# Rounded parts for two value projections and one value output product, with VectorE's sums made around them, in a cross-attention kernel on one Trainium2 core

## What is computed

```
Q = (img_embed @ Wq)          # 4096 x 512, heads of 512
K = (sent_embed @ Wk)         # 2 x 77 rows of 384
V = (sent_embed @ Wv)
score = einsum('bhqd,bhkd->bhqk', Q, K) / sqrt(512)
attn = softmax(where(mask, score, -inf))
ctx = einsum('bhqk,bhkd->bqhd', attn, V)
out = ctx @ Wo + img_embed
out = (out - mean) * rsqrt(var + 1e-5) * gamma + beta
```

## Time and profile before

| | us |
|---|---|
| median of 3 runs | 355.23 |
| profiled execution | 355.34 |
| its span in the trace | 353.3 |
| TensorE matmul busy | 347.6 (98%) |
| TensorE weight load busy | 324.0 (92%) |
| VectorE busy | 278.0 (79%) |
| ScalarE busy | 233.9 (66%) |
| GpSimd busy | 192.8 (55%) |

### The profile page before, as it was taken

The page is one execution under the profiler, slowest core; times in us unless marked ns, Lnnn a source line. Parts: engine busy times, 40 slices in busy tenths (PEclk is TensorE's granted clock), DMA queues, the critical chain, the costliest instruction groups (busy, mean ns, idle before and its releaser), DMA issues. The chain is left out here.

```text
span 353.3 us, 6822 instructions
## 1 busy us (share of the span) xinstructions
PE 347.6 (98%) x2272; PEld 324.0 (92%) x2272; DVE 278.0 (79%) x513; ACT 233.9 (66%) x784; POOL 192.8 (55%) x208
## 2 busy tenths in 40 slices
PE   9999999999999999999999999999999999999994
PEld 6999999999999999998899899989988998999884
DVE  2159999579756468898798988987987989889896
ACT  3267764254555669877876976878778769768560
POOL 0045650000003857689669688688696796885243
PEclk9999999999999999999999999999999999999998
DMA  7998769875635070053242341441522423413012
GB/s 250 414 420 316 272 225 339 262 267 221 217 131 220 0 283 17 4 178 105 76 160 63 136 151 46 164 144 38 179 97 83 151 70 138 149 42 110 32 47 103
DMA packets 19683, 55.80 MB, mean 158 GB/s; under 512 B 1729, under 2 KB 3265, under 8 KB 17729
## 3 DMA queue, kind: packets, MB, share of 16 engines
q1 hardware_dynamic: 18784, 54.38, 42.6%
q10 hardware_dynamic: 864, 1.00, 0.9%
HBM read 46.98 MB, written 8.39 MB: 157 GB/s over the span
## 5 line engine op out<-in xcount | busy, mean ns | idle before, releaser
L663 PE MATMUL pair<-vw_hi,pt_hi 128*128 128x512 f32 x155 | 62.3, 402 | 0.0
L663 PE MATMUL pair<-vw_hi,pt_lo 128*128 128x512 f32 x155 | 60.8, 393 | 0.0
L663 PE MATMUL pair<-vw_lo,pt_hi 128*128 128x512 f32 x155 | 60.6, 391 | 0.0
L1281 POOL TENSOR_TENSOR out_sb<-centred,beta_sb 128x512 f32<-128x512 f32 x30 | 38.8, 1294 | 29.0 <-ACT centred L857 28.9
L1301 POOL TENSOR_TENSOR x_sum<-xt_in 128x256 f32<-128x256 f32 x16 | 11.9, 745 | 62.2 <-DMA xt_in<-x_tiles 62.0
L812 ACT ACTIVATE prob<-c,neg_max 128x77 f32<-128x77 f32 x128 | 43.9, 346 | 0.0
L1326 POOL TENSOR_TENSOR xo_lo<-x_sum,xo_hi 128x512 fp32r<-128x512 f32 x32 | 41.4, 1298 | 0.5 <-ACT xo_hi L836 0.5
L588 PE MATMUL pair<-a_hi,xo_hi 128*128 128x308 f32 x128 | 40.4, 315 | 0.0
L588 PE MATMUL pair<-a_hi,xo_lo 128*128 128x308 f32 x128 | 38.9, 304 | 0.0
L588 PE MATMUL pair<-a_lo,xo_hi 128*128 128x308 f32 x128 | 38.9, 304 | 0.0
L1123 DVE TENSOR_TENSOR pair<-pair,x_in 128x512 f32<-128x512 f32 x31 | 21.7, 699 | 21.0 <-PE pair L663 20.7
(11 more groups left out here) (120 smaller groups left out, 992.7 us busy)
## 6 DMA issues: line engine op xcount, KB each, us to landing
w_out<-wo SPq DMA_DIRECT2D x8, 1024.0 KB, 4.8
xt_in<-x_tiles SPq DMA_DIRECT2D x16, 512.0 KB, 3.9
x_in<-x_rows SPq DMA_DIRECT2D x16, 512.0 KB, 4.8
out<-out_sb SPq DMA_DIRECT2D x31, 256.0 KB, 2.2
w_out<-wq_t SPq DMA_DIRECT2D x7, 1024.0 KB, 7.5
w_proj<-wv SPq DMA_DIRECT2D x8, 768.0 KB, 4.7
w_proj<-wk SPq DMA_DIRECT2D x6, 768.0 KB, 9.2
w_out<-wq_t SPq DMA_DIRECT2D x2, 512.0 KB, 7.5
```

What stands on the lines that cost most here:

```text
L663: mm = pe.matmul(ps_out[:, i % 2, 0:s.model], ps[:, j, :], v[:, b, j, :], start=(j == 0 and n == 0), stop=(j == s.key_t - 1 and n == len(p ...
L1281: pool.tensor_tensor(out_sb[i % OUT_RING][:, :], centred[i % 2][:, :], beta_sb[:, :], ALU.add)\
```

## The change

Projections 8 and 9 (values 0 and 1) and output product 8 are now done of rounded parts. `SPLIT_VALUES` gains use 8 (`H`), and projections are whole again from use 10 (`FROM_FULL`) instead of 8. Output product 9 stays whole although its projection comes in two pieces, so VectorE adds the second piece to `v_t` (`add_kv`), and TensorE waits for that sum (`dve_kv_sum`). VectorE makes T1 of batch 0 ahead of those additions and T1 of batch 1 behind them; T2 follows after output product 8's additions. ScalarE and GpSimd run their existing helpers for the added uses.

```
-    SPLIT_VALUES = range(H + 4, USES - 1)
+    SPLIT_VALUES = (H, *range(H + 4, USES - 1))
+    FROM_FULL = H + 2
...
-            return u < FULL_PROJ or u >= H
+            return u < FULL_PROJ or u >= FROM_FULL
...
+        def summed_kv(u):
+
+            return whole_out(u) and not whole(u)
...
             def wait_kv(u, half):
 
-                if whole_out(u):
+                if summed_kv(u):
+                    pe.wait_ge(dve_kv_sum, 2 * sum(summed_kv(v) for v in range(u)) + half + 1)
+                elif whole_out(u):
                     pe.wait_ge(act_kv_hi, 2 * u + half + 1)
...
+            def add_kv(u):
+
+                for half in range(2):
+                    values = value_of(u)[:, 2 * half:2 * half + 2, :]
+                    dve.wait_ge(act_kv_hi, 2 * u + half + 1)
+                    dve.tensor_tensor(values, second(ps_proj[half]), values, ALU.add).then_inc(dve_kv_sum, 1)
...
             for u in range(USES):
+                if u == H:
+                    right_sum(T1, 0)
                 if u + 1 < USES and not whole_out(u + 1):
                     split_kv(u + 1)
+                elif u + 1 < USES and summed_kv(u + 1):
+                    add_kv(u + 1)
+                if u == H:
+                    right_sum(T1, 1)
...
-                for n, task in {H: ((T1, right_sum), (T2, right_sum)), H + 1: ((T1, split_t), (T4, right_sum)),
+                for n, task in {H: ((T2, right_sum),), H + 1: ((T1, split_t), (T4, right_sum)),
...
-            for u in range(FULL_PROJ, H):
+            for u in range(FULL_PROJ, FROM_FULL):
```

More of the change, by code:

```diff
@@ L252, in build @@
         dve_comb, dve_half_max = sem("dve_comb"), sem("dve_half_max")
-        dve_vw_sum = sem("dve_vw_sum")
+        dve_vw_sum, dve_kv_sum = sem("dve_vw_sum"), sem("dve_kv_sum")
         dve_centred, dve_pad, dve_last = sem("dve_centred"), sem("dve_pad"), sem("dve_last")
```

## The result

| | before | after |
|---|---|---|
| median of the executions timed side by side, us | 355.3 (354.82 to 355.81, 6) | 356.8 (356.34 to 356.99, 6) |
| profiled execution, us | 355.34 | 356.77 |
| its span, us | 353.3 | 354.9 |
| last matmul of the program starts, us | 348.10 | 349.72 |

The ratio is 1.004 (95% interval 1.0027 to 1.0053): slower by 1.5 us. The forecast was 357.2 in a range of 356.0 to 358.4.

A forecast was written before the change was run, and what follows sets the result against it. TensorE was taken to bound the kernel, its saving swallowed by a wait for VectorE's vw_lo. Profiled 355.34 + 1.9 = 357.25, from the median 357.1; forecast 357.2 us, range 356.0 to 358.4.

The forecast's parts named there:

- TensorE's saving: Two split projections 0.24, one split output product 0.17, one mode change 0.02: TensorE spared 0.43 us at most.
- The 2.6 us: By the skill's four-pass rule the 40 replaced products would save 2.6 us on TensorE; the prediction kept the trace's 0.43.
- Step 1: VectorE's w_out_lo pairs, uses 6 and 7: with GpSimd newly working beside them, 3.50 us instead of 2.27.
- Step 2: VectorE, use 7: full rounds of 7.09 us move the instruction at 66.11 to 68.61, a delay of 2.50 us.
- Step 3: VectorE, use 8: four additions put among the T1 and T2 sums cost 1.29 us, bounds 1.2 and 1.92.
- Step 4: VectorE, end of T2: the splitting of T1 starts at 79.23 instead of 77.20, remaining delay 2.03 us.
- Step 5: VectorE from 77.20 to vw_lo: no idle time, so the vw_lo subtractions end at 91.66 instead of 89.63.
- The term +1.9: TensorE, second half of projection 12: waits for vw_lo and goes on at 91.74 instead of 89.81, +1.9 us.
- The short waits: Projection 10 waits for kv(9)'s sum (72.50 against 72.23); output product 9 finds its sums about on time; total unchanged.
- The clock rival: In TensorE's stall the granted clock falls too, costing 1.8 us or more: 359.1 us; chance 0.12.
- Not slower: GpSimd doesn't hold VectorE's w_out_lo: vw_lo 0.55 late, TensorE 0.4, 355.7 us; chance 0.12 with the still faster cases.

The follow-up runs named there:

- experiments 3 and 4: Changed kernel, each: GpSimd clearing w_proj_lo of projections 8 and 9 (355.56 us); vw_lo ahead of one sum plus v_t additions ahead of T1 (354.54 us).
- Experiment 3: Changed kernel with GpSimd writing zeros into w_proj_lo of projections 8 and 9 instead of subtracting: 355.56 us, ratio 1.0012.

## Why the prediction was right, step by step

- **TensorE's saving, 0.43.** It measured 0.42: from projection 7 to projection 12 TensorE takes 37.20 us before and 36.78 in the two kernels that have all the new products and no wait for `v_t` (experiments 3 and 4). In the changed kernel it takes 37.04, as 0.26 is given back in front of projection 10. (Projection 12 starts 0.26 us earlier on the clock of the span, but 0.10 of that is an earlier start of the whole chain.) The 2.6 us that the prediction worked out from the Trainium skill ("FP8 and Floating Point Precision", TensorE Precision Notes) showed in none of the versions without a wait for `vw_lo` (354.84, 354.54, 354.73): by it they would have come near 352.6. For the whole product the four passes fit: 4 x 154 columns at 2.4 GHz are an estimated 0.257 us, and its row gives 0.262. It is the rounded pair that the estimate had too cheap: 462 columns at one a cycle would be an estimated 0.193 us, and it takes 0.253.
- **Step 1, GpSimd's hold.** From the start of the pair to the next instruction 3.45 and 3.49 us, where 3.50 was forecast; the first instruction took 2400 ns. Experiment 3 shows that it is GpSimd's instruction, and that about 1.1 us of the run hang on it. The Trainium skill ("SBUF — State Buffer", Who interferes with whom) says that a VectorE instruction with two inputs in SBUF contends with a GpSimd instruction that reads SBUF, and that the shared ports are an exclusive lock. The trace agrees as to the contention: `w_out_lo` took 2400 ns where GpSimd was still subtracting, and both instructions of a pair together 2.35 us where it wasn't. No run here sets GpSimd's reading apart from its writing.
- **Step 2, the round.** 68.44 - 61.36 = 7.08 (7.09 forecast). The instruction of 66.11 came at 68.44, forecast 68.61. Most of the difference, 0.12, is an earlier start of the whole chain: the first `w_out_lo` pair of the stretch stood at 50.81 instead of 50.93.
- **Step 3, the inserted additions.** T2's last sum moved from 74.72 to 78.25, that is 3.53, less the 2.33 from step 2: 1.20. Forecast 1.29, lower bound 1.2. The additions kept the whole overlap that their neighbours have. (The bounds of this step, 1.2 and 1.92, give times of 357.1 to 357.8, and not the 356.9 to 357.9 that the prediction adds up to; the range was wide enough not to hang on it.)
- **Step 4.** `t_lo` at 78.97, a delay of 1.77 where 2.03 was forecast: the two terms above.
- **Step 5.** `vw_lo` ended at 91.37 (forecast 91.66) and projection 12 went on at 91.49 (91.74). The slack was 0.06 and not 0.15, which changes nothing, as the sum doesn't use it. The term +1.9 measured +1.68 there (+1.78 without the earlier start of the chain), +1.62 at the last matmul and +1.5 in the medians. This term of the sum was a little too large. Of the 0.4 by which the forecast missed the median, 0.25 arose here (91.74 against 91.49: 0.17 from step 2 and 0.09 from step 3); the rest is no more than what two executions of one kernel differ by.
- **The short waits.** The one in front of projection 10 costs 0.26, where 0.27 was forecast (72.50 - 72.23); none costs anything at output product 9.
- **The clock rival** (0.12, 359.1). It didn't happen in the changed kernel: PE's wait of 1.7 us left the clock at 1.00. It may have stood closer than a chance of 0.12 says, since a wait of 2.6 us in the same place took it down. The price was right in size: 1.8 or more in the prediction, 1.7 for the 3.4 us at half speed. One of its grounds is weaker than it reads: for the first 4 us of the span the granted clock column gives 1.00, so that the eight matmuls ran at the lower level rests on their 0.45 us alone.
- **Not slower** needed a GpSimd that doesn't hold VectorE. Experiment 3 is that case, and gives 355.56 where the rival said 355.7: 0.4 over its own before, with `vw_lo` 0.63 late (88.98 against 88.35) where the rival had 0.55.

## What to carry to other kernels

An engine near its limit pays for what it is made to wait, not for what its helpers do: walk the helper's list from the added work to the next thing that the limiting engine asks for, and subtract each idle gap on the way. Two edits that each fit under the same idle time can fail together. Here moving one block of work behind the awaited instruction took away the whole loss of 1.5 us, and with a second move there was a gain of 0.6 (0.2 to 0.9). Ask also whether a third engine, idle until now, will hold the helper when it gets work.

## What the runs showed of the hardware

- **The clock can fall after the stall.** With a wait of 2.6 us the granted clock stayed at 1.00 until 1.1 us after work had begun again, and was then 0.50 for 3.4 us. With a wait of 1.7 us (the changed kernel) nothing fell; with 5.5 us it fell 0.8 us before work began again, and 6.0 us were worked at 0.50. These are one trace each. A stall may thus cost well over its own length: 2.9 us of delay cost 4.55.
- **The place of the code moves the end.** With two programs that differ in 16 VectorE waits at the start, the last store landed in 2.8 or in 1.7 us, and the medians were 355.85 and 354.73. That is more than the whole saving of this change, and a reason to look at the last store before believing in a fraction of a per cent.
- **Rounded parts hardly save here.** A pair of passes with 308 and 154 columns takes 0.253 us, a whole float32 product of 154 columns 0.262.
